# The second expert layer's token rows: by a scatter to a row per expert and rank, with direct block loads and another turn order in phase C

## The reference, cut to what matters

```python
flat = x.reshape(B * T, D)                                   # 4096 tokens, D = 256
logits = flat @ router_w.T + router_bias
scores = softmax(logits)
topk_scores, topk_idx = top_k(scores, 4)
topk_scores = topk_scores / clip(topk_scores.sum(-1), 1e-12)
h = silu(einsum('nd,ehd->neh', flat, gate_w)) * einsum('nd,ehd->neh', flat, up_w)   # h = 128
expert_out = einsum('neh,edh->ned', h, down_w)
out = (take(expert_out, topk_idx) * topk_scores).sum(1)
out = out + silu(flat @ sgate_w.T) * (flat @ sup_w.T) @ sdown_w.T                   # shared expert
```

## Time and profile before

| | us |
|---|---|
| timed runs, median of 3 (lowest, highest) | 4344.7 (4343.72, 4346.62) |
| the profiled execution, its own time | 4317.87 |
| its span in the trace | 4316.1 |
| D, from its first transfer's issue at 3806.05 to the end | 510.1 |
| of it: ahead of the first block's matmuls at 3891.2 | 85.2 |
| of it: the last gathers, 4148.45 to 4309.06 | 160.6 |

### The profile page before, as it was taken

How to read it: one execution, slowest core, us unless ns; L and a number is a source line. 1 busy time by engine, 2 the same in 40 slices (tenths; PEclk the granted TensorE clock), 3 DMA queues, 4 the chain that set the end, 5 groups by cost and what they waited for, 6 DMA issues and landing times. The chain is left out here.

```text
span 4316.1 us, 78135 instructions
## 1 busy us (share of the span) xinstructions
PE 3976.5 (92%) x29168; PEld 2824.2 (65%) x29168; DVE 2323.2 (54%) x7158; ACT 1772.2 (41%) x3733; POOL 945.7 (22%) x1118
## 2 busy tenths in 40 slices
PE   7999999999999999999998899988999998769996
PEld 4666666666666666666665589966666666438963
DVE  4555655565556655665554522125566666474445
ACT  4455555555555455545542211113444444313420
POOL 2221222122212221222120011111000000005667
PEclk9999999999999999999999999999999999879998
DMA  3000000000000000000000169940000100029964
GB/s 114 1 4 9 8 6 4 9 8 6 3 9 8 6 4 9 8 6 4 6 13 33 74 237 333 332 165 13 30 23 26 31 21 11 13 71 299 335 200 143
DMA packets 136623, 284.25 MB, mean 66 GB/s; under 512 B 19968, under 2 KB 90176, under 8 KB 127680
## 3 DMA queue, kind: packets, MB, share of 16 engines
q1 hardware_dynamic: 84944, 200.03, 13.3%
q0 software_dynamic: 18336, 50.09, 4.0%
q10 hardware_dynamic: 32976, 29.13, 2.0%
HBM read 229.12 MB, written 50.07 MB: 65 GB/s over the span
## 5 line engine op out<-in xcount | busy, mean ns | idle before, releaser
L466 POOL TENSOR_SCALAR a_wide_p<-a_wide_p,a_w_inv 128x512 f32<-128x512 f32 x512 | 355.3, 706 | 1438.8 <-DVE a_w_inv L1133 1438.8
L903 ACT ACTIVATE a_wide_p<-a_wide_p,a_row_min 128x512 f32<-128x512 f32 x512 | 363.4, 713 | 114.0 <-DVE a_row_min L1128 112.5
L1203 DVE TENSOR_REDUCE a_q_pad<-ring 128x4 f32<-128x1024 f32 x256 | 301.1, 1219 | 87.5 <-PE ring L696 87.4
L1128 DVE CUSTOM_DVE_ANT_0 a_wide_p<-ring,a_neg_keys 128x512 f32<-128x512 f32 x403 | 266.0, 688 | 125.0 <-PE ring L550 124.8
L550 PE MATMUL ring<-a_qk 64*128 64x512 f32 x806 | 289.1, 643 | 21.6 <-DVE a_row_min L1128 15.0
L960 ACT ACTIVATE a_probs<-ring 128x1024 f32<-128x1024 f32 x256 | 250.5, 1019 | 72.6 <-PE ring L710 72.6
L1621 PE MATMUL ring<-b_xgt,b_we 128*128 128x128 f32 x2016 | 235.7, 275 | 0.5 <-DVE b_xgt L1784 0.5
L1621 PEld LDWEIGHTS ring<-b_xgt,b_we 128*128 128x128 f32 x2016 | 230.2, 192 | 1.1 <-DVE b_xgt L1784 0.7
L2689 DVE CUSTOM_DVE_ANT_0 c_junk<-ring,c_neg_mask 128x256 f32<-128x256 f32 x512 | 181.4, 420 | 89.3 <-PE ring L2219 89.3
L529 PE MATMUL acc<-a_kv_t,shared_w 128*128 128x512 f32 x392 | 196.0, 623 | 1.2 <-ACT a_kv_t L894 1.2
L1550 POOL DMA_INDIRECT d_xg<-d_rows,d_token_idx x159 | 150.1, 944 | 178.6 <-PE ring L1610 102.3
(11 more groups left out here) (464 smaller groups left out, 8547.3 us busy)
## 6 DMA issues: line engine op xcount, KB each, us to landing
b_we<-in_experts SPq DMA_DIRECT2D x63, 1536.0 KB, 9.3
d_we<-in_experts SPq DMA_DIRECT2D x159, 256.0 KB, 4.6
d_results<-d_yb ACTq DMA_DIRECT2D x159, 128.0 KB
b_results<-b_yb ACTq DMA_DIRECT2D x63, 128.0 KB, 9.0
a_cb<-in_ctx SPq DMA_DIRECT2D x16, 256.0 KB, 2.8
b_turned<-a_heads_t SPq DMA_DIRECT2D x16, 256.0 KB
b_rows<-a_heads SPq DMA_DIRECT2D x16, 256.0 KB
shared_x<-b_turned SPq DMA_DIRECT2D x8, 512.0 KB, 5.7
```

What stands on the lines that cost most here:

```text
L466: ins = pool.tensor_scalar(wide_p[:, h % 4, t, :], wide_p[:, h % 4, t, :], w_inv[:, t, h:h + 1], 1.0, ALU.mult, ALU.mult)
L903: ins = act.activation(wide_p[:, h % 4, t, :], wide_p[:, h % 4, t, :], ACT.Exp, scale=-1.0, bias=row_min[:, h, t:t + 1], accum_out=row_sum ...
L1128: dve.tensor_tensor_reduce(wide_p[:, h % 4, t, :], wbank(name), neg_keys[w % 2][:], -0.125, 3.0e38, ALU.add, ALU.min, row_min[:, h, t:t + ...
L1203: dve.tensor_reduce(q_pad[:, :, 2 * i:2 * i + 2, HD].rearrange("p t h -> p h t"), s, AX.X, ALU.max, negate=True).then_inc(nr.taken(name), 1)
```

## The change

Three things are changed together.

- **Scatter in C.** There is one DRAM tensor `d_cells` of 33 x 4096 rows. When a batch's ranks are known, DVE makes slots = expert x 4096 + rank, and GpSimd scatters the batch's rows to these places, 8 indirect transfers per batch. The store to `d_rows` goes. `c_x_e` has two buffers now, the second in the mask's tile `c_mask_i`. Since padding rows are read too, SP clears all of `d_cells` in A, by 66 transfers of 2 MB, 5 per batch from the third turn on.
- **D without a search.** A block's rows are 128 neighbours in `d_cells`. DVE works out each block's first row (`block_rows`). SP reads it into a register for each block and issues the load (`rows_in`); ACT reads it too, to store the results over the same rows. `places`, `make_pairs`, `find_tokens` and the gathers at L1550 are gone. Only group 0 of the shared expert stands ahead of the blocks (`early` is 1), 7 groups behind.
- **Turn order in C.** PE, ACT and DVE have some of their calls in another order.

The experts' rows and the output are turned ahead of the queries, the logits stand ahead of the first group by query, and less stands between the first and the second group. The core of the diff:

```diff
 # A, SP
+                            if i == 2:
+                                sp.wait_ge(made, 6)
+                            for n in range(5 * (i - 2), min(5 * (i - 1), cleared)) if i >= 2 else ():
+                                sp.dma_start(cells.rearrange("(n p m) d -> n p m d", p=P, m=16)[n],
+                                             neg_keys[0][:, 256:512].unsqueeze(1).to_broadcast([P, 16, D])).then_inc(cells_cleared, 16)
 # C, GpSimd
+                        def scatter(b):
+                            pool.wait_ge(e_placed, b + 1)
+                            for t in range(2):
+                                for k in range(rd.K):
+                                    pool.indirect_dma_start(out=cells, out_offset=bass.IndirectOffsetOnAxis(ap=rd.slots[:, k, 2 * b + t:2 * b + t + 1], axis=0),
+                                                            in_=x_e[b % 2][:, t, :], in_offset=None).then_inc(e_scattered[b % 2], 16)
                         for i in range(-4, B + 3):
+                            if on(i - 3):
+                                scatter(i - 3)
 # C, PE's order
-                            if on(n):
-                                pe.wait_ge(n_queries, n + 1)
-                                n_turn_queries(("Q", n))
-                            if on(n - 1):
-                                n_turn_out(n - 1)
-                            if on(n - 2):
-                                e_turn(n - 2)
+                            if on(n - 2):
+                                e_turn(n - 2)
+                            if on(n - 1):
+                                n_turn_out(n - 1)
+                            if on(n):
+                                pe.wait_ge(n_queries, n + 1)
+                                n_turn_queries(("Q", n))
...
-                            if on(x1):
-                                x_context(x1)
                             if on(n + 1):
                                 n_keys(n + 1)
...
                                 n_turn_queries(("Q2", n))
                             if on(x1):
+                                x_context(x1)
                                 x_turn(x1)
 # C, ACT's order: the output of the batch is copied at the turn's end, no more at the next one's start
-                            if on(n - 1):
-                                n_values_out(n - 1, 1)
+                            if on(n):
+                                n_values_out(n, 1)
 # C, DVE: e_apply, e_shares and route_choose stand ahead of x_products; n_values_in ahead of n_heads; and
+                            dve.scalar_tensor_tensor(out=rd.slots[:, :, 2 * b:2 * b + 2], in0=rd.choice[:], scalar=float(T * P),
+                                                     in1=rd.rank[:, :, 2 * b:2 * b + 2], op0=ALU.mult, op1=ALU.add).then_inc(e_placed, 1)
 # D, SP
+                        def rows_in(u):
+                            row = sp.value_load(block_rows[u % P:u % P + 1, u // P:u // P + 1], min_val=0, max_val=CELLS - P)
+                            if u >= XB:
+                                rg.wait_full(sp, ("x", u - XB))
+                            sp.dma_start(xg[:, u % XB, :], cells[bass.ds(row, P), :]).then_inc(loaded[u % XB], 16)
+                        if finish:
+                            for u in range(XB):
+                                rows_in(u)
                         for u in range(NB):
+                            if finish and u >= XB + 3:
+                                rows_in(u - 3)
 # D, ACT
+                                row = act.value_load(block_rows[u % P:u % P + 1, u // P:u // P + 1], min_val=0, max_val=CELLS - P)
+                                act.dma_start(r.results[bass.ds(row, P), :], yb[:, u % XB, :]).then_inc(stored[u % XB], 16)
 # D
-            expert_layer(rd, 128, gates[:, 7:8], a["experts3"], 0, 2, True)
+            expert_layer(rd, 128, gates[:, 7:8], a["experts3"], 0, 1, True)
```

More of the change, by code:

```diff
@@ L1490, in expert_layer @@
                 ring_order += [("sgu", u, i) for u in range(early, G) for i in range(4)] * finish
-                acc_order = [("total",), ("inverse",)] + [("dn", t) for t in range(4 * first, 4 * early)] + [("y", u) for u in range(NB)]
+                acc_order = [("total",)] + [("inverse",)] * (not finish) + [("dn", t) for t in range(4 * first, 4 * early)] + [("y", u) for u in range(NB)]
                 acc_order += [("dn", t) for t in range(4 * early, T)] * finish
@@ L1526, in _ @@
                             sp.dma_start(we[:, u % WB, :], w_experts[bass.ds(e, 1), :, 0:WS].rearrange("o p n -> (o p) n")).then_inc(weighted[u % WB], 16)
-                        for u in range(early, G):
+                        if finish:
+                            for u in range(NB - 3, NB):
+                                rows_in(u)
+                        for u in range(first + 2, G):
                             rg.wait_full(sp, ("sgu", u - 2, 3))
@@ L1594, in shared_out @@
                             ins.then_inc(ac.full(name), 1)
[L1596 to L1604 removed]
+                        if finish:
+                            for i in range(4):
+                                shared_in(first, i)
+                        else:
+                            for n in range(8):
+                                shared_in(first + n // 4, n % 4)
+                                for c in range(chunks * n // 8, chunks * (n + 1) // 8):
+                                    find_tokens(c)
+                            for u in range(first + 2, early + 2):
+                                for i in range(4):
+                                    shared_out(4 * (u - 2) + i)
+                                    if u < early:
+                                        shared_in(u, i)
                         def rows(u):
@@ L1635, in down @@
                             ins.then_inc(ac.full(("y", u)), 1)
-                        rows(0)
                         if finish:
+                            for i in range(4):
+                                shared_out(4 * first + i)
                             pe.wait_ge(downs_loaded, 16)
                             pe.wait_ge(experts_ready, 1)
+                        rows(0)
                         for u in range(NB):
@@ L1800, in _ @@
                                 ac.wait_taken(dve, ("dn", t))
-                            for u in range(early, G + 2):
+                            for u in range(early, early + T // 4):
                                 for i in range(4):
@@ L1901, in build @@
                     x_order += [(n, b) for n in ("cD", "cN", "simc", "sim", "best", "AT", "hq", "bcol", "hbar", "qv")]
[L1902 removed]
+                    n_order += ([("O", b - 1)] if b else []) + [("Q", b)] + [("S", b, i) for i in range(8)]
                     n_order += ([("cT", b + 1)] if b + 1 < B else []) + [("Q2", b)] + [("T", b, i) for i in range(8)]
@@ L1930, in build @@
                     e_chosen = sem(ctx, "c_e_chosen")
-                    e_rows_stored = sem(ctx, "c_e_rows_stored")
+                    e_placed = sem(ctx, "c_e_placed")
+                    e_scattered = [sem(ctx, f"c_e_rows_scattered{i}") for i in range(2)]
                     e_turned_stored = sem(ctx, "c_e_turned_stored")
@@ L2031, in _ @@
                                 root(x_norm, x_asked, x_given, i + 4)
+                        for j in range(2):
+                            pool.wait_ge(e_scattered[j], 16 * 2 * rd.K * (B // 2))
                     @block.tensor
```

160 lines of the change are left out of this document (91 added, 69 removed).

## The result

The changed kernel takes 4455.8 us (median of 4 runs, 4448.8 to 4461.2), the kernel before 4344.2 beside it: 1.0263 times, 95% interval 1.0251 to 1.0275. The forecast was 4370, 26 us more than before; it became 111 more.

The account below looks back on a forecast made before the run. Before, PE bounds C, and PE and DMA fill D's blocks; after, SP's queue bounds the blocks. D +38, C's order -29, scatter +17, clear 0 sum to +26 us on 4344.7, say 4370 us; range 4340 to 4415.

Parts of the forecast that it names:

- the mechanism of D's blocks: In D's blocks SP's two pairs of register load and issue set 2.24 us per block, before 1.59; 95 us lost.
- D's head: Start of D: without the search the first block can start at 27 us, before 85.2; gain 58 us.
- the clear: In A, 66 transfers of 2 MB on SP's queue cost 0, bounds 0 and +8 us.
- the order: In C the new turn order shortens PE's waits by 2.0 to 2.2 us per batch: -29 us, bounds 0 and -53.
- the tail: End of D: the gathers still end last, beside 7 shared groups; +1 us, bounds 0 and +8.
- 27 us above that execution, for no reason the trace shows: Whole kernel: the timed median lies 27 us above the profiled execution; the forecast put the difference on the median.
- the scatter at C's end: At C's end nothing hides the indirect writes, so D starts later: +17 us, bounds +12 and +27.
- In a full turn they lie between the rank and the next norm's root, beside the maxima, and cost nothing: In C's full turns eight indirect writes per batch, 10 us on GpSimd, are hidden and cost nothing.
- (a): Rival in D's blocks: SP is not the bound, blocks keep 1.59 us; kernel 4276 us, chance 0.08.
- (b): Rival: the forecast's mechanism with C's gain near its upper bound and a cheap end; +8 us, chance 0.12.
- (c): Rival in C: the new order wins nothing, the wait just moves; +58 us, 4403 us, chance 0.08.
- (d): Rival in D's blocks: PE's clock is 1.2 GHz, 90 us more, 4460 us, chance 0.04.

Follow-up runs that it names:

- e3_no_scatter: The changed kernel without the eight indirect writes per batch in C and their waits, so the routed part is missing from its output; 4360.2 us.
- e2_order: The kernel before with only the new turn order in C (PE, ACT and DVE); 4306.1 us, ratio 0.9919.

## Why the prediction was right or wrong

**Right: the mechanism of D's blocks.** SP's two pairs set the pace, as argued from the 2.56 us piece of the earlier trace rows. The size was off by a little: 2.30 to 2.31 in all profiles of it where it said 2.24, since the pair with the weights takes 1.22 in place of 1.11. From the first block to the gathers it is 4258.4 - 3886.9 = 371.5 us; the forecast had 352. That term was mis-sized by 20 us, within its bound of 2.5 per block. The Trainium skill's floor of about 600 ns for a tensor_load (DMA: Bandwidth & Descriptors, Latency and other measured facts) stays contradicted: the medians are 276 and 277 ns.

**Right: D's head**, 26.1 us against 27 forecast. **Right: the clear**, which delayed nothing: C begins at 2856.8 us, before at 2858.1.

**Right in sign, too low: the order**, -37 and -38 us in two comparisons against -29, both on kind A.

**Right, once chips of one kind are compared: the tail.** On kind B it is 160.9 us in the changed kernel (4183.6 to 4344.5) and 161.6 in the one before: the forecast said +1. Of the 26.6 us more that the two profiles show, 20 to 21 come from setting a trace of kind B against one of kind A, as the same D code shows; the other 5 or so may be the change's, and lie within its bound of +8. The prediction had a sign of this in hand, its "27 us above that execution, for no reason the trace shows". It put that down to nothing and was lucky in this: the shift is in both timed medians and drops out of their difference.

**Right in size: the scatter at C's end.** From the last mark to D's start it was 3806.05 - 3793.0 = 13 us in the kernel before, and is 3786.4 - 3753.4 = 33 on kind B and 33 on kind A too, so +20 against +17. The last 24 writes leave GpSimd in three bursts, 1.27 us from one to the next, the last at 3777.6. D starts 8.8 us later, where the forecast had 3 for landing and the barrier.

**The step that failed: "In a full turn they lie between the rank and the next norm's root, beside the maxima, and cost nothing".** It asked whom the writes keep waiting on GpSimd's own queue, and on that queue it was right: no root waits there for a write. It did not ask what the writes do to another engine. On kind A PE's semaphores are late while they go out, and the 6.4 us per turn of C (54.6 against 48.2) are the 5.0 us by which the maxima start late, and 1.7 us at the low clock that follows (the next two groups' maxima come 5.10 and 4.91 us after the last ones', where `e3_no_scatter` has 4.16), of which 0.3 is won back. The marks of C make that 757.4 - 681.5 = 76 us, and with 18 at the end of C it is the 94 us that `e3_no_scatter` gives. No row of before could show it: that trace was of the kind on which no late update was seen, and the kernel before has no indirect writes.

On kind B, the kind of that trace, the terms add up to -37 + 20 - 58 + 113 - 1 = +37 us against a measured +43 (interval 25 to 57 us): order, end of C, head, blocks, tail. The -37 is taken over from kind A; the order alone was not run on B. There the forecast of +26 was too low by its blocks (18) and its scatter (3), too high by its order (8) and tail (2). So on kind B the difference came out within the range, which reaches from 5 us less to 70 more than the 4344.7. On kind A the hold adds some 74 (the 94 of the scatter less 20), which carries the result past the upper end.

Of the rivals, (a) fell, since the pair does not overlap with anything; (b) fell, since blocks and the end of C both cost more than forecast; (c) fell by `e2_order`; (d) fell: the granted clock in the blocks is 0.97 with PE busy 76 of 100 us. That (d)'s 4460 lies next to the measured 4456 is chance. None of them was what happened.

## What to carry to other kernels

Cost a transfer on a queue not only by whom it delays there. On each of three chips of kind A, and on neither of two of kind B, a burst of indirect writes made PE's semaphores late, and then it counts against the slack of whoever waits for PE. Here it paid to break it up, four and four at two places of the turn in place of eight, 83 us. A register load and an issue cost SP's queue 1.1 to 1.2 us, so a queue that does two such pairs per block can't keep up with blocks of 1.6 us. And a profile is of one chip: where the profiled execution lies outside the spread of the timed ones, as 4317.9 did under 4343.7 to 4346.6, profile again before putting the difference down to noise.

## What the hardware showed that was not expected

- On chips of kind A, PE's semaphores arrive late while GpSimd issues indirect writes: by up to 5.8 us under eight in a row (10.0 us), by 0.3 to 1.3 under four (4.9 us), on time under eight plain ones (4.4 us). DVE's update inside the burst of eight was on time. On kind B PE's are on time under eight indirect ones. What distinguishes the chips, and what in the indirect writes does it, was not settled.
- The same 128 gathers take 161 to 163 us on kind B and 182 to 188 on kind A, with medians of 946 to 949 ns for one on both. Whether it is the same hold was not shown.
- An indirect write costs GpSimd's queue 0.97 us and 0.30 between two, about the same as a gather (0.95); a plain one 0.55.
